# First attention stage in head pairs on 32-row groups, and projection weights issued from ScalarE's queue

## The chip, the core and the metric

The kernel runs on one core of one Trainium2 chip. The metric is the device time of one execution in microseconds (us).

## What is computed

Two blocks with a residual and a layer norm before each, on x of 16 sequences x 256 positions x 128 features. The first is causal attention with 16 heads of 8 features. The second applies 6 layers; each is windowed attention (window 32, 16 heads of 64, normalised q and k, rotary tables) and a gated feed-forward with an inner norm, both on shifted tokens.

```python
def attn(x, Wq, Wk, Wv, Wo):
    B, S, E = x.shape
    H, D = 16, 8
    proj = lambda W: jnp.einsum('bse,fe->bsf', x, W).reshape(B, S, H, D).transpose(0, 2, 1, 3)
    q, k, v = proj(Wq), proj(Wk), proj(Wv)
    s = jnp.einsum('bhsd,bhtd->bhst', q, k)
    s = jnp.where(jnp.triu(jnp.ones((S, S), dtype=bool), k=1), -jnp.inf, s)
    a = jax.nn.softmax(s / sqrt(D), axis=-1)
    out = jnp.einsum('bhst,bhtd->bhsd', a, v).transpose(0, 2, 1, 3).reshape(B, S, E)
    return jnp.einsum('bse,fe->bsf', out, Wo)

x = x + attn(layernorm(x), Wq, Wk, Wv, Wo)
y = layernorm(x)
for i in range(6):
    y = window_attn(shift(y), Wqkv[i], q_scale[i], k_scale[i], Wo[i]) + y
    y = gated_ffn(shift(y), ln_g[i], ln_b[i], W1[i], b1[i], W2[i], b2[i]) + y
x = x + y
```

## The kernel before

Each of the five engines has its own program, an order of work written out by hand, and semaphores tie them together: `need(eng, sem, value)` makes an engine wait until `sem` has reached `value`. Engines work strictly in the order of their programs. SyncE (SP) mostly issues DMAs.

**First stage.** `attention_steps` runs a pipeline over the 16 sequences. In step n, sequence n is at its head (norm, turn, projections), sequence n - 1 in the middle (scores to values), n - 2 at the tail (output, residual, norm). Steps 2 to 15 are one hardware loop. For the middle, 16 heads are taken in four groups of four, g = 0 to 3. `a_scores` puts one group's scores in PSUM: a bfloat16 matmul of the identity with the causal mask opens each of three banks (lines 1023, 1026), then for each head one matmul with the first 128 queries against 128 keys (L1030) and one with the last 128 queries against 256 keys (L1034). The stationary side is AqT, all 128 features; the moving side is KM, which holds for each head a copy of the keys with the features of the other heads set to zero. GpSimd makes KM with `spread_k` (L363) from AkT and the head mask. VectorE takes the maxima (`a_max`, L732 and L733), ScalarE the exponentials (`a_exp`, L500 and L502), TensorE turns them in 12 blocks of 128 x 512 (`a_transposes`, L1053), in two PSUM slots, and ScalarE copies blocks 0 to 5 (L513), VectorE blocks 6 to 11 (L743), to SBUF. Then come the values (`a_values`, L1063 and L1068), and `a_divide` on VectorE: transpose (L748), reciprocal, multiply over all 1024 elements (L753), transpose (L756). The output matmuls (L1075) and the residual (L761) belong to the next step. PSUM has two sets of three banks for the scores; the second also takes the values (banks 3, 4) and the output (bank 5).

For the next sequence, `a_turn` (L999), `a_x_evac` (L478), `a_project` (L1005), `a_qk_evac` (AqT at L483, AkT at L485) and `a_project_v` (L1010) stand between these. Their PSUM space is that of the two block slots, so block 3 waits for a_xe and block 4 for a_ke, the copy of AkT. TensorE's order in a step is:

```python
            def a_step(n, head, mid, tail):
...
                if head:
                    if mid:
                        need(pe, a_te, 12 * n - 12 + 3)
                    a_turn(n)
                    a_project(n)
                if mid:
                    a_scores(n - 1, 3)
                    for g in range(1, 4):
                        a_transposes(n - 1, g, head)
                    a_values(n - 1)
```

**Layers.** `stack_steps` runs the same kind of pipeline over 6 x 16 units of one sequence. At a layer's end the weights must be replaced: `load_qkv` on SyncE (L241) brings Wqkv in three parts of 512 KB, v, q and k, in the last unit's step, behind that step's `band` (L281, L283, L287) and `edge_values` (L296) DMAs, each part once s_pv, s_pq or s_pk says that the last projection with it is done. The projections are L1136; ScalarE copies their results with L568 (squares) and L575 (`keep_raw`) for q and k and L588 for v.

**Start.** SyncE issues the first inputs, weights and constants, then the load of all other inputs, and then, after GpSimd has cleared Wap, the four parts of Wap (L237). TensorE waits for all of `d_c` (5 constants) and `d_wa` (7 loads, Wap's among them) before its first instruction.

## Time and profile before

| | us |
|---|---|
| median of 3 runs (lowest to highest) | 4052.52 (4048.25 to 4054.8) |
| the profiled execution | 4053.12 |
| its span in the trace | 4051.3 |
| TensorE matmul busy | 3611.0 (89%) |
| VectorE busy | 3103.8 (77%) |
| ScalarE busy | 2876.5 (71%) |
| GpSimd busy | 2423.2 (60%) |
| first projection matmul of the layers (end of the first stage) | 544.8 |
| mean granted TensorE clock | 0.983 of full |

The span is the time from the first to the last instruction in the trace; the execution's own time is 1.8 us longer. Busy shares are means over the whole span, and a step with a chain of waits through several engines can be long while no engine in it is full. Durations of pipelined instructions overlap: what one costs in a row of its like is the distance between starts.

### The profile page before, as it was taken

The page shows a single profiled execution, that of the slowest core. Times are in us where ns is not written, and L with a number is a line of the kernel's source. Part 1 is how long each engine was busy: PE and PEld are TensorE (multiplying, and loading weights), DVE is VectorE, ACT ScalarE, POOL GpSimd, SP SyncE. Part 2 cuts the span into 40 slices and gives each one's busy share as a digit, 9 for nine tenths or more (in the row PEclk, how much of TensorE's full clock was granted, in tenths as well). Part 3 has the DMA queues.
Part 4 walks back from the last instruction along what each step waited for, and adds up shares of the span by engine and source line. Part 5 has one row for each costly group of instructions (what it writes and reads, how often), then busy time and mean ns, then how long its engine had stood idle before and what let it go on. Part 6 is the DMA issues. An engine that isn't in the chain of part 4 may idle for free.

```text
span 4051.3 us, 97145 instructions
## 1 busy us (share of the span) xinstructions
PE 3611.0 (89%) x34144; PEld 2541.3 (63%) x34144; DVE 3103.8 (77%) x5305; ACT 2876.5 (71%) x4769; POOL 2423.2 (60%) x1603
## 2 busy tenths in 40 slices
PE   6888869999889999899999899999899998999997
PEld 5666646666566666566666566666666665666665
DVE  4656658888778888778888778888788887888885
ACT  3554447777677777677777677777677776777775
POOL 3222246666666666666666666666566665667663
PEclk9999989999999999999999999999999999999998
DMA  1000001111111111111111111111211111111111
GB/s 56 0 0 0 0 12 34 32 32 34 52 41 31 35 35 35 50 38 35 35 34 36 46 42 35 34 35 35 53 35 35 34 34 44 47 35 35 34 33 48
DMA packets 183169, 136.82 MB, mean 34 GB/s; under 512 B 97612, under 2 KB 135888, under 8 KB 182992
## 3 DMA queue, kind: packets, MB, share of 16 engines
q1 hardware_dynamic: 182992, 134.51, 13.7%
q8 instruction: 104, 1.70, 0.2%
q14 instruction: 73, 0.60, 0.1%
...
## 4 chain that ended last, share of the span: by engine, by line
PE 50%; DVE 14%; ACT 11%; SPq 11%; issue 7%; DMA 5%; POOL 1%; DVEq 0%; ACTq 0%; POOLq 0%
PE ps L1136 9%; PE ps L1177 9%; PE ps L1189 8%; SPq L281 5%; PE ps L1230 5%; PE ps L1215 4%; DMA BD<-area 3%; PE ps L1204 3%; PE ps L1240 3%; SPq L283 3%; DVE area L820 3%; ACT kbd L599 2%; DVE lsum L810 2%; DVE mx L799 2%; DVE area L804 2%
## 5 line engine op out<-in xcount | busy, mean ns | idle before, releaser
L1136 PE MATMUL ps<-Wqkv,xsT 128*128 128x512 f32 x2304 | 1124.0, 611 | 93.1 <-DMA Wqkv<-ffn_Wqkv 44.5
L418 POOL TENSOR_TENSOR area<-area,tab 128x512 f32<-128x512 f32 x384 | 490.1, 1276 | 829.9 <-ACT area L575 829.9
L1136 PEld LDWEIGHTS ps<-Wqkv,xsT 128*128 128x128 f32 x2304 | 406.0, 193 | 432.8 <-issue 337.2
L432 POOL TENSOR_TENSOR area<-area,lsum 128x1024 f32<-128x1024 f32 x192 | 365.3, 1903 | 336.1 <-DVE lsum L813 336.1
L568 ACT ACTIVATE area<-ps 128x1024 f32<-128x1024 f32 x384 | 393.6, 1025 | 202.6 <-PE ps L1136 200.4
L419 POOL TENSOR_TENSOR area<-area,tab 128x512 f32<-128x512 f32 x384 | 490.0, 1276 | 0.0
L426 POOL TENSOR_TENSOR AQb<-AQb,area 128x1024 f32<-128x1024 f32 x192 | 449.8, 2365 | 7.5
L426 POOL TENSOR_TENSOR area<-area 128x1024 f32<-128x1024 f32 x192 | 450.5, 2370 | 0.0
L1177 PE MATMUL ps<-BD,area 128*64 128x128 f32 x6144 | 420.3, 279 | 20.8 <-DMA BD<-area 10.1
L1189 PEld LDWEIGHTS ps<-Wo,area 128*128 128x128 f32 x3072 | 375.9, 193 | 94.5 <-issue 93.6
L1177 PEld LDWEIGHTS ps<-BD,area 128*64 128x64 f32 x6144 | 337.3, 138 | 133.3 <-DMA BD<-area 80.1
L1129 PE MATMUL ps<-xnT,W 128*128 128x256 f32 (+1 forms) x1152 | 289.7, 388 | 120.9 <-DVE H L826 119.4
L605 ACT ACTIVATE area<-ps 128x512 f32<-128x512 f32 x384 | 210.5, 609 | 263.3 <-PE ps L1215 263.3
L575 ACT ACTIVATE area<-ps 128x1024 f32<-128x1024 f32 x384 | 392.8, 1023 | 0.0
L1230 PE MATMUL ps<-kbd,area 128*32 128x128 f32 x12288 | 377.8, 275 | 0.0
L1189 PE MATMUL ps<-Wo,area 128*128 128x128 f32 x3072 | 376.4, 276 | 1.5 <-ACT area L612 1.5
L1230 PEld LDWEIGHTS ps<-kbd,area 128*32 128x32 f32 x12288 | 325.9, 110 | 81.4 <-issue 81.3
L1129 PEld LDWEIGHTS ps<-xnT,W 128*128 128x128 f32 (+1 forms) x1152 | 198.4, 179 | 272.7 <-DVE H L826 198.3
L873 DVE TENSOR_TENSOR AQb<-area,ps 128x1024 f32<-128x1024 f32 x192 | 232.8, 1212 | 151.9 <-ACT area L575 151.9
L612 ACT ACTIVATE area<-ps 128x512 f32<-128x512 f32 x384 | 230.4, 600 | 158.6 <-PE ps L1182 113.2
L363 POOL TENSOR_TENSOR area<-AkT,headmask 128x4096 f32<-128x4096 f32 x16 | 112.4, 7027 | 373.6 <-ACT AkT L485 373.6
L820 DVE STREAM_TRANSPOSE area<-area 128x1024 f32<-128x1024 f32 x192 | 238.1, 1240 | 72.6 <-POOL area L432 72.6
...
## 6 DMA issues: line engine op xcount, KB each, us to landing
...
x2s<-x2s SPq DMA_DIRECT2D x96, 7.5 KB, 2.0
```

The source lines that it names most:

```text
L418: pool.tensor_tensor(b4[:, :, 0:h], q4[:, :, h:DH], s4[:, :, 0:h], ALU.mult).then_inc((s_bq, s_bk)[j], 1)
L419: pool.tensor_tensor(b4[:, :, h:DH], q4[:, :, 0:h], s4[:, :, h:DH], ALU.mult).then_inc((s_bq, s_bk)[j], 1)
L426: pool.tensor_tensor(AQ[t][:, col], AQ[t][:, col], BQ[:, col], ALU.add).then_inc(s_rot, 1)
L432: pool.tensor_tensor(p3, p3, lsum[:, 1, :].unsqueeze(2).broadcast_to([P, HEADS, 2 * WIN]), ALU.mult).then_inc(s_pn, 1)
L568: act.activation(SQ[:, j * INNER:(j + 1) * INNER], PJ[:, :], ACT.Square).then_inc((s_sqq, s_sqk)[j], 1)
L575: act.activation(QH[:, j * INNER:(j + 1) * INNER], PJ[:, :], ACT.Copy).then_inc((s_hq, s_hk)[j], 1)
L820: dve.transpose(PTr[t][:, :, :, :].rearrange("p b h i -> p h b i"), Pr[:, t, :]).then_inc(s_T, 1)
L1129: last = mm(TR[c % 2][0:m, half * SEQ:(half + 1) * SEQ], W1[:, half * FF + f0:half * FF + f0 + m], xnT[:, :], start=True, stop=True)
L1136: last = mm(PJ[:, b * 512:(b + 1) * 512], xsT[:, par, t * P:(t + 1) * P], Wqkv[:, w0:w0 + 512], start=True, stop=True)
L1177: last = mm(slot[DH * k:DH * k + DH, c * P:(c + 1) * P], V[par][:, t, h * DH:(h + 1) * DH], BD[:, t, :, h, :], start=(c == 0), stop=False, ...
L1189: last = mm(EXO[:, t * P:(t + 1) * P], oT[:, t, c, :], Wo[:, c, :], start=(c == 0), stop=(c == PAIRS - 1))
L1230: last = mm(SC[32 * w:32 * w + 32, c // 4, (c % 4) * P:(c % 4 + 1) * P], qT[:, c, 32 * w:32 * w + 32], kbd[:, c, :, k0:k0 + 2 * WIN], star ...
```

## The change

The first stage works on pairs of heads. The four heads of a 32-row group g are h = 4g + k, k = 0 to 3, and pair j takes head k = j // 2 of two groups, g = 2 (j % 2) and the next. Each head's score matmul contracts only the 32 rows of its group, and the two of a pair write different banks. KM therefore needs four copies instead of 16 (with `slotmask`, the head mask cut to four columns). Three sets of two banks are used in turn, values and output moving to banks 4 and 5. The mask matmul covers the 256 columns that need one. Blocks are now those of one k over the four groups; ScalarE copies four of them and VectorE eight, with a semaphore each. AqT and KM exist twice. The multiply of `a_divide` covers 8 of 32 rows of each block. Wqkv is loaded from ScalarE's program. At the start, the identity comes first, Wap and the remaining inputs later, the rotary tables last, with semaphores of their own, and GpSimd clears kbd and BD after the first KM.

```diff
-        KM = area3[:, :].rearrange("p (h k) -> p h k", h=HA)
+        KM = area3[:, 0:2048].rearrange("p (b k n) -> p b k n", b=2, k=4)
         area4 = sb("area4", [P, 2048])
         PT1 = area4[:, :].rearrange("p (h q) -> p h q", h=HA)
+        P0k = area2[:, :].rearrange("p (g k q) -> p k g q", g=4, k=4)
+        P1k = area4[:, :].rearrange("p (g k q) -> p k g q", g=4, k=4)
...
-            a_step(0, True, False, False)
-            a_step(1, True, True, False)
-            with eng.Fori(2, SEQS) as n:
-                a_step(eng.snap(n), True, True, True)
-            a_step(SEQS, False, True, True)
-            a_step(SEQS + 1, False, False, True)
-
+            a_step(0, 0, True, False, False)
+            a_step(1, 1, True, True, False)
+            with eng.Fori(0, SEQS // 2 - 1) as k:
+                for odd in range(2):
+                    a_step(eng.snap(2 * k + (2 + odd)), odd, True, True, True)
+            a_step(SEQS, 0, False, True, True)
+            a_step(SEQS + 1, 1, False, False, True)
+
+
+        PAIRS_A = HA // 2
+        TE_ACT, TE_DVE = 4, 8
+
+        def pair_bank(j):
+            return 2 * (j % 3)
+
+        def pair_heads(j):
+            return [(2 * (j % 2) + b, j // 2) for b in range(2)]
 
         def block_slot(i):
             return TR[i % 2] if i < 3 else TR[(i + 1) % 2]
 
         def block_home(i):
 
-            h = slice(i // 3 * 4, i // 3 * 4 + 4)
-            return (PT0[:, h, 0:P], PT0[:, h, P:SEQ], PT1[:, h, :])[i % 3]
+            k = i // 3
+            return (P0k[:, k, :, 0:P], P0k[:, k, :, P:SEQ], P1k[:, k, :, :])[i % 3]
+
+        def block_done(n, i):
+
+            return (a_te, TE_ACT * n + i + 1) if i < TE_ACT else (a_td, TE_DVE * n + i - TE_ACT + 1)
...
+            sp.dma_start(ident[:, :], c_ident).then_inc(d_c, 16)
             sp.dma_start(xres[:, 0:early, :], x_rows[:, 0:early, :]).then_inc(d_x, 16)
             for i, w in enumerate((wq_t, wk_t, wv_t)):
                 sp.dma_start(Wa[:, i, :], w).then_inc(d_wa, 16)
-            for src, dst in ((c_ident, ident[:, :]), (c_causal, causal_f[:, :]),
-                             (c_winmask, wmask_f[:, :, :]), (c_headmask, headmask[:, :]),
-                             (c_rot, rot[:, :, :, :])):
+            for src, dst in ((c_causal, causal_f[:, :]), (c_winmask, wmask_f[:, :, :]), (c_headmask, headmask[:, :])):
                 sp.dma_start(dst, src).then_inc(d_c, 16)
 
-            sp.dma_start(xres[:, early:, :], x_rows[:, early:, :]).then_inc(d_x2, 16)
             sp.wait_ge(i_pad, 2)
             wo_rows = wo_t.rearrange("(c g d) n -> g d c n", g=4, d=DA)
             for g in range(4):
-                sp.dma_start(Wap[32 * g:32 * g + DA, :, :], wo_rows[g]).then_inc(d_wa, 16)
-
-            def load_qkv(l, part, done):
-                col = slice(part * INNER, (part + 1) * INNER)
-                sp.dma_start(Wqkv[:, col], wqkv[l][:, col]).then_inc(done, 16)
...
-                if at == SEQS - 1:
-                    need_apart(sp, i_sp, s_pv, (layer + 1) * SEQS * TILES)
-                    load_qkv(layer + 1, 2, d_wv)
-                    need_apart(sp, i_sp, s_pq, (layer + 1) * SEQS * TILES)
-                    load_qkv(layer + 1, 0, d_wq)
-                    need_apart(sp, i_sp, s_pk, (layer + 1) * SEQS * TILES)
-                    load_qkv(layer + 1, 1, d_wk)
...
+            def spread_k(n, par):
                 need(pool, a_ke, n + 1)
-                need(pool, a_s, 4 * n)
-                pool.tensor_tensor(KM[:, :, :], AkT[:, :].unsqueeze(1).broadcast_to([P, HA, SEQ]),
-                                   headmask[:, :].unsqueeze(2).broadcast_to([P, HA, SEQ]), ALU.mult).then_inc(a_km, 1)
-
-            spread_k(0)
-            with pool.Fori(1, SEQS) as n:
-                spread_k(pool.snap(n))
+                need(pool, a_s, PAIRS_A * (n - 1))
+                pool.tensor_tensor(KM[:, par, :, :], AkT[:, :].unsqueeze(1).broadcast_to([P, 4, SEQ]),
+                                   slotmask[:, :].unsqueeze(2).broadcast_to([P, 4, SEQ]), ALU.mult).then_inc(a_km, 1)
+
+            def a_step(n, par, head, mid, tail):
+                if head:
+                    spread_k(n, par)
+                    if isinstance(n, int) and n == 0:
+                        pool.memset(kbd[:, :, :, :], 0.0).then_inc(i_zero, 1)
+                        pool.memset(BD[:, :, :, :], 0.0).then_inc(i_zero, 1)
+
+            attention_steps(pool, a_step)
...
+            def load_qkv(l, part, done):
+                col = slice(part * INNER, (part + 1) * INNER)
+                act.dma_start(Wqkv[:, col], wqkv[l][:, col]).then_inc(done, 16)
...
+            def a_exp(n, j):
+                if j == 0:
                     need(act, a_t, 12 * n)
-                need(act, a_mx, 4 * n + g + 1)
-                bank = 3 * (g % 2)
-                for h in range(4 * g, 4 * g + 4):
-                    k = h - 4 * g
-                    act.activation(E0[:, h, :], ps[:, bank, k * P:(k + 1) * P], ACT.Exp,
-                                   bias=nmx[:, 0, h:h + 1])
-                    last = act.activation(E1[:, h, :], ps[:, bank + 1 + k // 2, (k % 2) * SEQ:(k % 2 + 1) * SEQ], ACT.Exp,
-                                          bias=nmx[:, 1, h:h + 1])
+                need(act, a_mx, PAIRS_A * n + j + 1)
+                for b, (g, k) in enumerate(pair_heads(j)):
+                    h, bank = 4 * g + k, pair_bank(j) + b
+                    act.activation(E0[:, h, :], ps[:, bank, 0:P], ACT.Exp, bias=nmx[:, 0, h:h + 1])
+                    last = act.activation(E1[:, h, :], ps[:, bank, P:P + SEQ], ACT.Exp, bias=nmx[:, 1, h:h + 1])
                 last.then_inc(a_e, 1)
...
+            def a_step(n, par, head, mid, tail):
                 if mid:
                     a_exp(n - 1, 0)
+                    a_exp(n - 1, 1)
                 if tail:
                     rsqrt_guess(n - 2, b_lnc, b_lnr, b_lnr)
                 if mid:
-                    a_evac(n - 1, 0)
+                    a_exp(n - 1, 2)
+                    for i in range(3):
+                        a_evac(n - 1, i)
                 if head:
                     rsqrt_guess(n, a_lnc, a_lnr, a_lnr)
                 if mid:
-                    a_exp(n - 1, 1)
+                    a_exp(n - 1, 3)
                 if head:
                     a_x_evac(n)
                 if mid:
-                    a_exp(n - 1, 2)
-                if head:
-                    a_qk_evac(n)
-                if mid:
-                    a_evac(n - 1, 1)
-                    a_exp(n - 1, 3)
+                    a_exp(n - 1, 4)
+                if head:
+                    a_qk_evac(n, par)
+                if mid:
+                    a_evac(n - 1, 3)
+                    for j in range(5, PAIRS_A):
+                        a_exp(n - 1, j)
                 if head:
                     a_values(n)
 
             act.wait_ge(i_zero, 2)
             act.wait_ge(i_guess, 2)
+            load_qkv(0, 0, d_wq)
+            load_qkv(0, 1, d_wk)
+            load_qkv(0, 2, d_wv)
...
                     v_evac(n, 1, par)
+                    if again:
+                        load_qkv(layer + 1, 2, d_wv)
...
                     keep_raw(n, 1, 0)
+                    if again:
+                        load_qkv(layer + 1, 0, d_wq)
...
                     keep_raw(n, 1, 1)
+                    if again:
+                        load_qkv(layer + 1, 1, d_wk)
...
+            def a_max(n, j):
+
+                bank, (g, k) = pair_bank(j), pair_heads(j)[0]
+                hs = slice(4 * g + k, 4 * g + k + 5, 4)
+                need(dve, a_s, PAIRS_A * n + j + 1)
+                if j == 0:
+                    need(dve, a_e, PAIRS_A * n)
+                dve.tensor_reduce(nmx[:, 0, hs], ps[:, bank:bank + 2, 0:P], AX.X, ALU.max, negate=True)
+                dve.tensor_reduce(nmx[:, 1, hs], ps[:, bank:bank + 2, P:P + SEQ], AX.X, ALU.max, negate=True).then_inc(a_mx, 1)
+
+            def a_evac(n, i):
+
+                need(dve, a_t, 12 * n + i + 1)
+                dve.tensor_copy(block_home(i), block_slot(i).rearrange("p (h q) -> p h q", h=4)).then_inc(a_td, 1)
...
-                dve.tensor_tensor(o3, o3, Arl[:, :].unsqueeze(2).broadcast_to([P, 32, 32]), ALU.mult).then_inc(a_mu, 1)
+                heads = o3[:, :, 0:DA]
+                dve.tensor_tensor(heads, heads, Arl[:, :].unsqueeze(2).broadcast_to([P, 32, DA]), ALU.mult).then_inc(a_mu, 1)
...
+                    a_max(n - 1, 4)
+                    a_evac(n - 1, 4)
+                    a_max(n - 1, 5)
+                    a_evac(n - 1, 5)
+                    a_max(n - 1, 6)
+                    for i in range(6, 9):
+                        a_evac(n - 1, i)
+                    a_max(n - 1, 7)
+                    for i in range(9, 12):
+                        a_evac(n - 1, i)
...
+                if j >= 3:
+                    need(pe, a_e, PAIRS_A * n + j - 2)
+                bank = pair_bank(j)
                 for b in range(2):
-                    mm(ps[:, bank + 1 + b, :], ident_h[:, :], causal[:, :].unsqueeze(1).broadcast_to([P, 2, SEQ]),
-                       start=True, stop=False, skip_group_check=True)
-                for k in range(4):
-                    h = 4 * g + k
-                    mm(ps[:, bank, k * P:(k + 1) * P], AqT[:, 0:P], KM[:, h, 0:P],
-                       start=False, stop=True, skip_group_check=True)
-                for k in range(4):
-                    h = 4 * g + k
-                    last = mm(ps[:, bank + 1 + k // 2, (k % 2) * SEQ:(k % 2 + 1) * SEQ], AqT[:, P:SEQ], KM[:, h, :],
+                    mm(ps[:, bank + b, 0:3 * P].rearrange("p (a k) -> p a k", a=3)[:, 0:3:2, :], ident_h[:, :],
+                       causal[:, P:2 * P].unsqueeze(1).broadcast_to([P, 2, P]), start=True, stop=False, skip_group_check=True)
+                for b, (g, k) in enumerate(pair_heads(j)):
+                    r = slice(32 * g, 32 * g + 32)
+                    mm(ps[:, bank + b, 0:P], AqT[r, par, 0:P], KM[r, par, k, 0:P], start=False, stop=True, skip_group_check=True)
+                for b, (g, k) in enumerate(pair_heads(j)):
+                    r = slice(32 * g, 32 * g + 32)
+                    last = mm(ps[:, bank + b, P:P + SEQ], AqT[r, par, P:SEQ], KM[r, par, k, :],
                               start=False, stop=True, skip_group_check=True)
                 last.then_inc(a_s, 1)
...
+                if mid:
+                    a_scores(n - 1, 0, 1 - par)
+                    a_scores(n - 1, 1, 1 - par)
                 if tail:
                     a_output(n - 2)
                 if mid:
-                    a_scores(n - 1, 1)
+                    a_scores(n - 1, 2, 1 - par)
                     a_transposes(n - 1, 0, head)
-                    a_scores(n - 1, 2)
+                    a_scores(n - 1, 3, 1 - par)
                 if head:
                     if mid:
-                        need(pe, a_te, 12 * n - 12 + 3)
+                        need(pe, *block_done(n - 1, 2))
                     a_turn(n)
                     a_project(n)
                 if mid:
-                    a_scores(n - 1, 3)
-                    for g in range(1, 4):
-                        a_transposes(n - 1, g, head)
+                    a_scores(n - 1, 4, 1 - par)
+                    a_transposes(n - 1, 1, head)
+                    a_scores(n - 1, 5, 1 - par)
+                    a_scores(n - 1, 6, 1 - par)
+                    a_transposes(n - 1, 2, head)
+                    a_scores(n - 1, 7, 1 - par)
+                    a_transposes(n - 1, 3, head)
                     a_values(n - 1)
                 if head:
                     if mid:
-                        need(pe, a_te, 12 * n)
+                        need(pe, *block_done(n - 1, 11))
                     a_project_v(n)
```

TensorE, first stage, the step in which sequence 1 is at its head and sequence 0 in the middle, from the projections on, before (L1005 projections, L1023 to L1034 scores, L1053 block transposes, L1063 and L1068 values, L1010 projection of v):

```order
L1005 MATMUL ps<-xhT,Wa 128x256 x2
L1023 MATMUL ps<-causal,ident_h 128x512
L1026 MATMUL ps<-causal,ident_h 128x512 x2
L1030 MATMUL ps<-area,AqT 128x128 x4
L1034 MATMUL ps<-area,AqT 128x256 x4
L1053 MATMUL ps<-ident,area 128x128 x36
L1063 MATMUL ps<-area 32x256 x16
L1068 MATMUL ps<-area 32x128 x16
L1010 MATMUL ps<-Wa,xhT 128x128 x2
```

The same place in the changed kernel, from blocks 3 to 5 on (L1052 to L1059 scores of a pair, L1078 transposes, L1089 values); pair 4 stands just ahead of it:

```order
L1078 MATMUL ps<-ident,area 128x128 x12
L1052 MATMUL ps<-causal,ident_h 128x2x128 x2
L1056 MATMUL ps<-area,AqT 128x128 x2
L1059 MATMUL ps<-area,AqT 128x256 x2
L1052 MATMUL ps<-causal,ident_h 128x2x128 x2
L1056 MATMUL ps<-area,AqT 128x128 x2
L1059 MATMUL ps<-area,AqT 128x256 x2
L1078 MATMUL ps<-ident,area 128x128 x12
L1052 MATMUL ps<-causal,ident_h 128x2x128 x2
L1056 MATMUL ps<-area,AqT 128x128 x2
L1059 MATMUL ps<-area,AqT 128x256 x2
L1078 MATMUL ps<-ident,area 128x128 x12
```

Before, all scores stood ahead of the last 36 transposes; now three pairs of eight stand among them, pairs 5 and 6 behind block 5 and pair 7 behind block 8.

SyncE, the last step of a layer, before (L296 the edge values, L241 Wqkv, L302 and L303 the token shift):

```order
L296 DMA Vx<-area 32x2x128 [waits s_o]
L296 DMA Vx<-area 32x2x128 x3
L40 ISA
L241 ISA [waits s_pv]
L241 DMA Wqkv<-ffn_Wqkv 128x1024
L241 REGISTER_ALU [waits s_pq]
L241 DMA Wqkv<-ffn_Wqkv 128x1024
L241 ISA [waits s_pk]
L241 DMA Wqkv<-ffn_Wqkv 128x1024
L302 DMA x2s<-x2s 112x2x64 [waits s_r1]
L303 DMA x2s<-x2s 15x2x64
```

ScalarE, the same step in the changed kernel, around the load of q's part (L585 squares, L592 `keep_raw`, L578 gelu, L482 Wqkv):

```order
L585 ACTIVATE area<-ps 128x1024 [waits s_rq,s_pq]
L40 REGISTER_ALU
L592 ACTIVATE area<-ps 128x1024 [waits s_aq,s_bq]
L482 REGISTER_ALU
L482 DMA Wqkv<-ffn_Wqkv 128x1024
L40 REGISTER_ALU
L578 ACTIVATE G<-ps,b1s 85x256 [waits s_h]
L692 ACT_TABLE_LOAD
L585 ACTIVATE area<-ps 128x1024 [waits s_rk,s_pk]
```

The three loads have left SyncE's queue, and each now stands on ScalarE behind the copy of what the part's last matmuls wrote.

## Rows read from the trace of the kernel before

**Rows 1.** Timeline of one steady step of the first stage: start, duration, engine, line, [idle before]

```profile
151.54 1.93 PE L1063 MATMUL ps<-area 128*32 128x256 f32 x32 [0.78 <-DVE area L743]
156.08 1.22 DVE L753 TENSOR_TENSOR area<-area,Arl 128x1024 f32<-128x1024 f32 x1
161.46 0.38 PE L1023 MATMUL ps<-causal,ident_h 128*128 128x512 bf16 x1 [0.77 <-DVE x L761]
169.77 0.38 PE L999 MATMUL ps<-ident,xh 128*128 128x128 f32 x2
171.59 0.38 PE L1023 MATMUL ps<-causal,ident_h 128*128 128x512 bf16 x1
172.24 1.05 PE L1030 MATMUL ps<-area,AqT 128*128 128x128 f32 x8
173.13 1.89 PE L1034 MATMUL ps<-area,AqT 128*128 128x256 f32 x8
175.77 1.15 PE L1053 MATMUL ps<-ident,area 128*128 128x128 f32 x8 [0.31 <-ACT AkT L485]
180.18 1.09 PE L1053 MATMUL ps<-ident,area 128*128 128x128 f32 x8 [0.96 <-ACT area L502]
183.05 1.93 PE L1063 MATMUL ps<-area 128*32 128x256 f32 x32 [0.78 <-DVE area L743]
```

**Rows 2.** The same timeline: maxima, norm and exponentials in that step

```profile
165.41 0.66 DVE L732 TENSOR_REDUCE nmx<-ps 128x4 f32<-128x512 f32 x1
165.99 1.22 DVE L733 TENSOR_REDUCE nmx<-ps 128x4 f32<-128x1024 f32 x1
167.84 0.16 DVE L697 TENSOR_TENSOR lw<-lw 128x2 f32<-128x2 f32 x1 [0.64 <-ACT lw L472]
168.43 0.60 DVE L707 TENSOR_SCALAR xh<-xres,mv,lw 128x128 f32 x2
177.45 0.36 ACT L500 ACTIVATE area<-ps,nmx 128x128 f32<-128x128 f32 x1
178.06 0.38 ACT L500 ACTIVATE area<-ps,nmx 128x128 f32<-128x128 f32 x1
```

**Rows 3.** Timeline of TensorE in a layer: a change of tile shape

```profile
2020.15 0.59 PE L1225 MATMUL ps<-wmask,ident_h 128*128 128x512 bf16 x2
2020.68 1.95 PE L1230 MATMUL ps<-kbd,area 128*32 128x128 f32 x64
2022.56 1.09 PE L1215 MATMUL ps<-ident,AQb 128*128 128x128 f32 x8
...
2020.68 1.69 PEld L1230 LDWEIGHTS ps<-kbd,area 128*32 128x32 f32 x64 [0.42 <-issue]
```

**Rows 4.** First layer boundary; then all waits, landings, and a stretch with granted clock

```profile
1089.55 1.03 ACT L575 ACTIVATE area<-ps 128x1024 f32<-128x1024 f32 x1
1099.37 2.50 SPq L296 DMA_DIRECT2D Vx<-area  x4
1102.25 1.55 SPq L241 DMA_DIRECT2D Wqkv<-ffn_Wqkv  x3
1107.53 3.77 PE L1136 MATMUL ps<-Wqkv,xsT 128*128 128x512 f32 x4 [9.50 <-DMA Wqkv<-ffn_Wqkv]
1116.77 1.88 PE L1136 MATMUL ps<-Wqkv,xsT 128*128 128x512 f32 x4
...
PE ps L1136 <- DMA Wqkv<-ffn_Wqkv: 44.5, 5, 9.5
DMA to landing us min/median/max: 3.6/4.5/8.3
1107.00:1112.00 5.00, 4.47 (x9) 2.40 (x10) 0.00 (x0) 0.66 (x1) 0.00 (x0) 0.50 0.20 79
```

**Rows 5.** The start: timeline

```profile
16.66 0.66 PE L999 MATMUL ps<-ident,xh 128*128 128x128 f32 x2 [16.66 <-DMA Wap<-Wo_t]
20.70 7.02 POOL L363 TENSOR_TENSOR area<-AkT,headmask 128x4096 f32<-128x4096 f32 x1 [8.71 <-ACT AkT L485]
```

119 lines of the change are left out of this document (48 added, 71 removed).

## The prediction

> **What bounds the kernel now.** I read the page first: the first stage, which most of the diff touches, ends at about 544 of 4051 us. TensorE is the busiest engine, but what matters for a reordered stage is what it waits for, so I went to the timeline of one steady step of the first stage. One step runs from the start of the value matmuls at 151.54 to the same place at 183.05, 31.5 us [rows 1]. In it TensorE works through four score groups of 3.4 us (mask 171.59 to the end 173.13 + 1.89) and stands still where a wait ends last: for the residual at 161.46, for ScalarE's AkT at 175.77, for exponentials at 180.18, for a block copy at 183.05 [rows 1]. So the step is a chain through three engines. The second place is a layer boundary: the projection matmuls wait 44.5 us in five waits for Wqkv [rows 4]. The third is the start, where TensorE waits until 16.66 for the last Wap load [rows 5].
>
> Below, t counts from the start of the value matmuls of a step.
>
> **Cost of a pair of heads.** Before, a group of four heads has three mask matmuls (171.59 to 172.24, 0.65), four 128-column ones (to 173.13, 0.89) and four 256-column ones (1.89 with 0.17 of pipeline end, so 0.43 per head) [rows 1]. A pair now has one 512-column mask's worth of work in two halves, 0.21, then 2 x 0.22 and 2 x 0.43. The rows of before show no row group of 32, only column groups: 64 instructions (two per f32 matmul) in 1.95, about 28 ns each, where a 128-column instruction of the score group takes 110 (0.89 for eight): four run side by side [rows 1, 3]. If the two row groups do too, the multiplying takes 0.22 + 0.43 = 0.65. The weight loads may then bind: 64 loads of 32 columns took 1.69, 26 ns each, one behind the other [rows 3]; eight loads of 128 columns at four times that take 0.85. Changing the shape costs 0.53 - 0.43 = 0.10 on the way in (2020.15 to 2020.68 with two masks of 0.21) and about 0.15 on the way out (64 x 0.0267 after 2020.68 is 2022.39, the next starts at 2022.56) [rows 3]. Bounds of a pair: below, everything beside everything, 0.21 + 0.65 = 0.86 with free switches, 0.95 with the way in; above, nothing side by side, 0.21 + 0.10 + 0.44 + 0.86 = 1.6. I take 1.2, near the bound by loads (0.21 + 0.10 + 0.85 + the end of the last matmul), because loads are what the nearest rows show to be serial.
>
> A rule of the Trainium skill (TensorEngine Tiling, Tiling Modes) says that changing the tiling mode drains the engine; the 0.10 and 0.15 agree with it. By the page TensorE: Matmul & The Clock Gate, section LDWEIGHTS, a 32x128 load takes as long as a 128x128 one, an estimate of 107 ns x 8 = 0.86 here; the sum by it would be a pair of 1.27 and 5 us more in all.
>
> **Other new durations.** A reduce over 512 elements takes 0.58 until the next starts and one over 1024 takes 1.22, 1.1 ns an element [rows 2]; the new ones over 256 and 512 take 0.33 + 0.58 + 0.08 of end = 1.0 per pair. Exponentials take 0.61 per head (177.45 to 178.06), so 1.2 per pair and 0.1 of end [rows 2]. Newton and normalising take 1.2 (167.84 to 169.03), a block's copy of 512 elements is taken like the reduce, 0.6 [rows 2]. The multiply of the division shrinks from 1024 to 256 elements: 1.22 to 0.40 [rows 1].
>
> **The step, link by link.**
> 1. Values, division, output, residual: 161.46 - 151.54 = 9.9 before; the shorter multiply makes it 9.1. That multiply is on the path.
> 2. Pair 2 waits for this (its banks hold the output): end at 10.5, maxima 11.45, exponentials 12.8. ScalarE now has them ahead of the copy of block 0, so block 2 can be transposed only at 13.4, until 13.95.
> 3. Pair 3: end 15.4, maxima 16.3, normalising 17.5 (it stands behind this maximum on VectorE), then turn, copy, projections: 2.0, as from 169.77 to the mask at 171.59 with its load [rows 1]. t = 19.55; before 20.05.
> 4. Pair 4: end 20.95, maxima 21.9, exponentials 23.2, AqT and AkT 23.85, and block 4 starts at 23.9. Before, it started at 175.77, t = 24.2. Up to here nothing is lost.
> 5. Before, one group had yet to be exponentiated, and all scores were done; values began 7.3 later. Now pairs 5, 6 and 7 are still to be computed. Blocks 4 and 5 end at 24.9; pair 5 at 26.3, maxima 27.3, exponentials 28.75. Pair 6 hides beside these. Blocks 6 to 8 end at 30.8 (each waits for the copy two before it).
> 6. Pair 7 stands behind them on TensorE: end 32.25, maxima 33.2, exponentials 34.65. Blocks 9 to 11 and the last copy take 183.05 - 180.18 = 2.9 as before [rows 1]. Values at t = 37.5.
>
> So a step takes 6.0 us more, though TensorE computes 4 us less in it. With 16 sequences there are 15 such intervals: **+90**. Five pairs lie on the path, so 0.1 us on a pair is 0.5 on a step and 8 in all.
>
> **Start.** KM of 7.02 [rows 5] is computed over a quarter of the elements, 1.8: -5.2, once; in the steady step it ends long before it is needed, so doubling q and keys buys nothing there. TensorE waited for Wap until 16.66 [rows 5]; the new order needs only ident, the masks and three weights, so it can start when VectorE has normalised the first sequence. But ScalarE's 1.5 MB of Wqkv now run beside them. I take -4.5 (bounds 0 and -7). The later load of the other inputs is needed in step 1, some 25 us in: nothing. The memsets of kbd and BD move behind the first KM on GpSimd, beside idle time.
>
> **Layer boundaries.** SyncE issues all three Wqkv loads at 1102.25, behind a step's band and edge DMAs, and q's matmuls start at 1107.53 after 9.5 us of waiting, in a stretch with a granted clock of 0.50 (1.2 GHz): four instructions take 3.77 there and 1.88 in the next such place [rows 4]. On ScalarE, q's load is issued behind the copy of q's raw projection, 1089.55 + 1.03 = 1090.6; with 0.5 for the issue (three took 1.55) and 4.5 to landing it is there at 1095.6, and TensorE is ready for it at 1107.53 - 9.50 = 1098.0 [rows 4]. k's comes some 5 us later and is needed after another 6 us of matmuls. That gives back 44.5 + 5 x 1.9 = 54. The 15 issues now cost ScalarE up to 0.5 each, 7.8 in all, some of it on its path to TensorE: 4. **-50**, bounds -35 (landing at the slowest 8.3 [rows 4], issues fully seen) and -58 (the rest of those steps freed too).
>
> **Sum** against the profiled execution's 4053.1: +90 - 5.2 - 4.5 - 50 = +30, or 4083. The median of the runs, 4052.5, is the same within 0.02%. About 0.2%, 8 us, is what a measurement of this kernel can tell from no change.
>
> **Rivals.**
> - *TensorE's work decides, not the chain* (ends faster). Place: from block 4 to the values. Four groups of 3.4 become eight pairs of 1.2, 4.1 us less a step, if the maxima and exponentials of pairs 5 and 7 are hidden: 4053 - 62 - 60 = 3931. It decides against me from a lengthening under 4.0 us a step (60 / 15). For it: TensorE is the busiest engine. Against it: TensorE already waits there with only one group left, and each pair must pass two more engines. 8%, with the intermediate sizes.
> - *The row groups do not run side by side*: a pair is 1.6, a step 2.2 longer again, 4083 + 33 = 4116. For it: no row shows row groups. Against it: column groups do overlap. 14%.
> - *The loads come no earlier from ScalarE's queue.* Each boundary keeps its 9.5 us: 4083 + 50 = 4133. Against it: SyncE reached them straight from the edge loads (1099.37 + 2.50, then 1102.25) [rows 4], while their conditions had long been met; the wait is its order. The Trainium skill (Trainium Kernel Development and Optimization, Key Constraints) says that issuing from several engines saves only the sequencer's issue time; here that would be some 1.5 us a boundary. 4%.
> - *The change does only its small parts*, pairs at the lower bound and boundaries fully freed: 4083 - 20 - 8 - 3 = 4052, no change. 8%, with its neighbours.
> - My forecast, slower by 0.3 to 1.2%: 66%.
>
> The range, 4046 to 4121, takes in the lower bounds together and the rival of the row groups; outside lie most of the first rival and the third. Faster by over 0.2%: 0.11 (the first rival and 3 from the low end of the forecast); within: 0.10 (the fourth and 2 more); slower: 0.79.
>
> **What would show it.** A steady step of 36.5 to 38.5 between value matmuls, its length added after block 4; TensorE waiting 2.5 us before blocks 6 and 9 for exponentials; a pair of 1.0 to 1.3 on TensorE; no wait for Wqkv at the boundaries, the first projection at 11 to 13 us. I am wrong if a step stays under 35.5, or if Wqkv is still waited for.

## The result, and the profile after

The changed kernel took 4197.86 us (median of 4 runs, 4192.29 to 4205.28). The kernel before, on the same chip, took 4053.66 (4048.25 to 4059.97). The ratio is 1.0356, with a 95% interval from 1.0334 to 1.0378: slower by 144 us. Forecast were 4083 us and a range of 4046 to 4121. The direction was right, the size was not, and the time lies outside the range.

The profiled execution spans 4190.5 us. Its page begins so (busy time of each engine; then the span in 40 slices, PEclk being the granted clock in tenths):

```profile
span 4190.5 us, 97397 instructions
...
PE 3677.9 (88%) x34208; PEld 2530.5 (60%) x34208; DVE 3122.3 (75%) x5465; ACT 2868.7 (68%) x4737; POOL 2342.3 (56%) x1607
...
PE   6767767799999899998999989999989999999997
...
PEclk9777776899999999999999999999999999999998
```

Of the first seven slices of PEclk, some 730 us, the first reads 9, five read 7 and the last 6; behind them stand 8 and 9. These seven are the first stage. To see where it ends in each trace, take the first projection of the layers:

```profile
L1168 PE MATMUL ps<-Wqkv,xsT 128*128 128x512 f32 x2304 | 1121.0, 610 | 48.0 <-ACT area L592 43.6 <-ACT area L605 3.3 <-ACT xsT L567 1.0
```

The timeline gives this line's first start as 738.9 us, where before it was 544.8. So the account of the profiled executions is: first stage **+194.1**, layers 4190.5 - 738.9 = 3451.6 against 4051.3 - 544.8 = 3506.5, **-54.9**. The sum, +139.2, is what the two spans differ by.

**The layers.** In the row above no time is left behind a Wqkv transfer, where [rows 4] had 44.5 us. The loads now come from ScalarE's queue (from the view of the tile Wqkv):

```profile
L482 ACTq DMA_DIRECT2D Wqkv<-ffn_Wqkv x18: 345/357/453, 2.0 to 3560.9; - x18
```

The first boundary step, from the first matmul of one unit (the transpose of its input, L1145; L1113 before) to that of the next, takes 36.56 us (1219.42 to 1255.98), where before it was 47.0 (1095.60 to 1142.59): 10.4 saved; there are five boundaries.

**The first stage.** One steady step on TensorE, from the start of the value matmuls (the timeline: start, time, instruction, and in brackets the idle time before it and what ended it). It answers to [rows 1]:

```profile
151.25 3.55 PE L1089 MATMUL ps<-area 128*32 128x256 f32 x32 [0.88 <-DVE area L762]
...
156.16 0.38 PE L1052 MATMUL ps<-causal,ident_h 128*128 128x256 bf16 x2
156.47 0.49 PE L1056 MATMUL ps<-area,AqT 32*128 32x128 f32 x4
156.79 0.60 PE L1059 MATMUL ps<-area,AqT 32*128 32x256 f32 x4
157.32 0.39 PE L1052 MATMUL ps<-causal,ident_h 128*128 128x256 bf16 x2
...
162.00 0.39 PE L1052 MATMUL ps<-causal,ident_h 128*128 128x256 bf16 x2 [0.78 <-DVE x L781]
...
166.25 0.66 PE L1078 MATMUL ps<-ident,area 128*128 128x128 f32 x4 [1.98 <-ACT area L523]
...
170.20 0.69 PE L1028 MATMUL ps<-ident,xh 128*128 128x128 f32 x2 [2.22 <-DVE xh L731]
171.36 2.07 PE L1034 MATMUL ps<-xhT,Wa 128*128 128x256 f32 x4 [0.47 <-ACT xhT L495]
...
178.38 1.93 PE L1078 MATMUL ps<-ident,area 128*128 128x128 f32 x8 [2.48 <-ACT AkT L502]
...
184.68 2.56 PE L1078 MATMUL ps<-ident,area 128*128 128x128 f32 x12 [1.34 <-ACT area L517]
...
191.76 3.02 PE L1078 MATMUL ps<-ident,area 128*128 128x128 f32 x12 [2.52 <-ACT area L517]
...
195.66 0.65 PE L1089 MATMUL ps<-area 128*32 128x256 f32 x4 [0.88 <-DVE area L762]
```

The step is 195.66 - 151.25 = **44.4 us**, against 31.5 before and the 37.5 of the prediction. The starts of the value matmuls divide the stage's +194.1 in this way: -7.1 until the first score matmul (it starts at 20.72, and at 27.78 before), +11.9 from there to the first values (these start at 61.78, and at 56.97 before), +188.3 in the fifteen intervals between the first and the last values (the last one is shorter in both kernels and grew by 7.6 only), and +0.9 from the last values to the layers. Two things are to be seen in the step. Most waits have the places and the sizes of the prediction's walk: 2.52 us for exponentials before block 9, 2.48 for AkT before block 4. And instructions that the change did not touch take up to twice as long: the value matmuls 3.55 where they took 1.93 [rows 1], the eight transposes of blocks 4 and 5 1.93 where eight at full clock take 1.09 (163.18 in this same step), the projections 2.07 where they take 1.13 in the experiments below. The table by stretch says why (stretch, its length, busy time and instructions of PE, PEld, DVE, ACT and POOL, the granted clock, DMA share, GB/s):

```profile
151.25:155.00 3.75, 3.75 (x48) 2.15 (x52) 0.00 (x0) 0.00 (x0) 0.00 (x0) 0.56 0.02 4
155.00:160.00 5.00, 4.40 (x58) 3.04 (x48) 4.15 (x7) 0.38 (x1) 0.00 (x0) 1.00 0.01 2
160.00:165.00 5.00, 3.49 (x29) 2.52 (x28) 3.71 (x14) 3.84 (x13) 0.00 (x0) 1.00 0.00 0
165.00:170.00 5.00, 1.73 (x14) 1.10 (x14) 2.92 (x13) 3.68 (x12) 0.00 (x0) 0.82 0.00 0
170.00:175.00 5.00, 4.33 (x16) 2.69 (x16) 0.14 (x1) 0.82 (x3) 0.00 (x0) 0.50 0.00 0
175.00:180.00 5.00, 2.52 (x16) 2.04 (x13) 1.53 (x3) 2.39 (x7) 1.51 (x1) 0.84 0.00 0
...
185.00:190.00 5.00, 4.23 (x22) 2.64 (x19) 2.78 (x5) 1.16 (x4) 0.00 (x0) 0.53 0.00 0
190.00:195.70 5.70, 3.06 (x16) 2.36 (x19) 2.40 (x4) 1.36 (x4) 0.00 (x0) 0.50 0.00 0
```

The granted clock is 1.00 (2.4 GHz) from 155 to 165, where TensorE works without a long break. Then it waits 1.98 and 2.22 us, and from 170 to 175 the clock is 0.50 (1.2 GHz). It comes back, and is gone again from 185 on, into the value matmuls of the next step (the first line shows that place one step earlier). Before, the four stretches of 50 us from 50 to 250 all had 1.00. In the change such stretches have 0.70 to 0.76 from 100 us on, the lowest and the highest of them being:

```profile
100.00:150.00 50.00, 34.21 (x234) 22.82 (x230) 22.72 (x51) 16.54 (x48) 1.89 (x1) 0.70 0.00 0
...
200.00:250.00 50.00, 36.10 (x262) 24.19 (x258) 25.49 (x55) 16.76 (x49) 1.89 (x1) 0.76 0.00 0
```

**The start.** TensorE's first instruction comes at 14.72, against 16.66 [rows 5]. It no longer waits for Wap but for VectorE, which begins its part only when the last constant has landed. The copy of keys on GpSimd takes 1.89 against 7.02 [rows 5]:

```profile
11.35 0.23 DVE L736 CAST ident_h<-ident 128x128 bf16<-128x128 f32 x1 [11.35 <-DMA headmask<-const]
...
14.72 0.66 PE L1028 MATMUL ps<-ident,xh 128*128 128x128 f32 x2 [14.72 <-DVE xh L731]
...
18.77 1.89 POOL L370 TENSOR_TENSOR area<-AkT,slotmask 128x1024 f32<-128x1024 f32 x1 [6.34 <-ACT AkT L502]
```

### The profile page after: what moved, and what is told of

Same layout as the page of the kernel before. It is cut to its first block, busy times and chain, and to the rows that moved or that the text cites. A ratio compares the mean times of both kernels' runs of the same rounds, so it can differ in the third digit from the quotient of the medians.

```text
span 4190.5 us, 97397 instructions
## 1 busy us (share of the span) xinstructions
PE 3677.9 (88%) x34208; PEld 2530.5 (60%) x34208; DVE 3122.3 (75%) x5465; ACT 2868.7 (68%) x4737; POOL 2342.3 (56%) x1607
## 4 chain that ended last, share of the span: by engine, by line
PE 55%; DVE 15%; ACT 11%; SPq 7%; issue 7%; DMA 4%; POOL 1%; ACTq 0%; DVEq 0%; POOLq 0%
PE ps L1168 10%; PE ps L1209 9%; PE ps L1221 8%; PE ps L1262 5%; SPq L291 4%; PE ps L1236 4%; DMA BD<-area 4%; PE ps L1247 3%; PE ps L1272 3%; PE ps L1078 3%; SPq L293 2%; DVE area L849 2%; DVE lsum L839 2%; ACT kbd L616 2%; DVE mx L828 2%
## 5 line engine op out<-in xcount | busy, mean ns | idle before, releaser
L585 ACT ACTIVATE area<-ps 128x1024 f32<-128x1024 f32 x384 | 393.5, 1025 | 156.5 <-PE ps L1168 154.2
L592 ACT ACTIVATE area<-ps 128x1024 f32<-128x1024 f32 x384 | 392.6, 1022 | 0.0
L370 POOL TENSOR_TENSOR area<-AkT,slotmask 128x1024 f32<-128x1024 f32 x16 | 30.3, 1894 | 618.4 <-ACT AkT L502 618.4
L516 ACT ACTIVATE area<-ps,nmx 128x128 f32<-128x128 f32 x256 | 95.0, 371 | 303.9 <-DVE nmx L757 303.9
```

The lines of the kernel that those rows point to most:

```text
L585: act.activation(SQ[:, j * INNER:(j + 1) * INNER], PJ[:, :], ACT.Square).then_inc((s_sqq, s_sqk)[j], 1)
L592: act.activation(QH[:, j * INNER:(j + 1) * INNER], PJ[:, :], ACT.Copy).then_inc((s_hq, s_hk)[j], 1)
```

## The experiments

The question is what made a step 44.4 us and not 37.5, and what each other part was worth. Theories on the step, named in the expectations by letters: a longer chain with the lost clock on top; more work or slower work of TensorE itself (the 32-row form); something else in the new parts. Then: is it the form of the score matmuls or the order around them that costs, and can the order be mended?

### The weight loads alone

The kernel before, with only the issue of Wqkv moved to ScalarE's program: the three first loads ahead of its first stage, the others each behind ScalarE's copy of the last projection of their part.

```diff
-                if at == SEQS - 1:
-                    need_apart(sp, i_sp, s_pv, (layer + 1) * SEQS * TILES)
-                    load_qkv(layer + 1, 2, d_wv)
...
+                    v_evac(n, 1, par)
+                    if again:
+                        load_qkv(layer + 1, 2, d_wv)
...
+                    keep_raw(n, 1, 0)
+                    if again:
+                        load_qkv(layer + 1, 0, d_wq)
```

> The kernel before, with only the Wqkv loads moved to ScalarE's program. Theory A (loads issued earlier): the layers give back what they gave back in the changed kernel, 3506.5 to 3451.6 us, so about 55 us: 3995 to 4002 us, no wait of TensorE for Wqkv, first stage unchanged with 31.5 us a step. Rival (the gain of the layers came from something else in the change, such as the rotary tables or the clearing of BD): 4045 to 4055 us.

Measured: 4001.47 us (3993.4 to 4002.19), ratio 0.9878, interval 0.9862 to 0.9895. The profiled span is 3999.5, the first stage ends at 545.0, so the layers take 3454.5: **-52.0** of the change's -54.9. The steady step stays at 31.5. This part is a gain by itself, and the loss of the change is all in the rest. This is the time that the expectation gave. TensorE starts at 18.19 here, 1.5 later than in [rows 5], with 1.5 MB of Wqkv beside the first loads; the last experiments return to it. The first values come at 56.98, where they came at 56.97 before: matmuls near 30 us reached full clock sooner in this execution, and that hid the later start.

### Filling TensorE's waits

The changed kernel, with idle work for TensorE: 39 mask matmuls of 128 x 512 per step, into banks that are overwritten later, issued where it would wait (8 before block 2, 8 before the turn, 9 before block 4, 4 before block 6, 10 before block 9). They add work and take nothing away, so if this kernel is faster, the clock is what is left to explain it.

```diff
+            def fill(n, pairs, bank, count):
+                need(pe, a_e, PAIRS_A * n + pairs)
+                for _ in range(count):
+                    mm(ps[:, bank, :], ident_h[:, :], causal[:, P:2 * P].unsqueeze(1).broadcast_to([P, 4, P]),
+                       start=True, stop=True, skip_group_check=True)
...
+                if k == 2:
+                    fill(n, 5, 2, 4)
+                if k == 3:
+                    fill(n, 6, 4, 10)
...
+                    if i == 2:
+                        fill(n, 2, 2, 8)
+                    if i == 4:
+                        fill(n, 3, 4, 9)
...
+                        fill(n - 1, 2, 2, 8)
                         need(pe, *block_done(n - 1, 2))
```

> The changed kernel with 39 extra bfloat16 matmuls of the mask a step, placed in TensorE's five long waits of the first stage and written to banks that are free there. Theory B (the waits of the longer chain let the clock fall to half, and the half clock adds the 7 us a step that the forecast lacks): the granted clock stays at 1.00, a steady step takes 36.5 to 38.5 us although TensorE has 8 us more to do in it, and the time falls by about 15 x 7 = 105, to 4080 to 4110 us. Rival C (the clock falls because of the 32-row matmuls): granted clock stays near 0.7, a step takes 44 us or more, 4190 us or more. Rival D (the pair itself costs more): clock 1.00 but a step of 42 us or more.

Measured: 4077.5 us (4071.31 to 4081.01), ratio to the kernel before 1.007, interval 1.0053 to 1.0087. So 8 us of added matmuls a step made the changed kernel some 116 us faster (by the ratios; 120 by the medians). Its table by stretch, and a step on its timeline:

```profile
150.00:200.00 50.00, 43.58 (x340) 26.09 (x339) 27.38 (x60) 20.25 (x59) 3.79 (x2) 1.00 0.00 0
```

```profile
167.67 1.93 PE L1103 MATMUL ps<-area 128*32 128x256 f32 x32 [0.88 <-DVE area L762]
...
191.11 1.14 PE L1092 MATMUL ps<-ident,area 128*128 128x128 f32 x8 [0.53 <-ACT AkT L502]
...
198.94 2.33 PE L1066 MATMUL ps<-causal,ident_h 128*128 128x512 bf16 x10
201.53 1.09 PE L1092 MATMUL ps<-ident,area 128*128 128x128 f32 x8 [0.25 <-ACT area L517]
...
204.50 1.93 PE L1103 MATMUL ps<-area 128*32 128x256 f32 x32 [0.88 <-DVE area L762]
```

The granted clock is 1.00, the value matmuls are back at 1.93, and the step is 204.50 - 167.67 = 36.8 us, as expected (36.5 to 38.5; the total fell slightly below the expected 4080). The wait before block 9 is still there, only now it is filled: 2.33 us of added matmuls and 0.25 of waiting. So of the 12.9 us that a step grew, **5.3 are the longer chain and 7.6 the half clock**. Over the whole stage, which ends at 623.4 here, 78.6 of the 194.1 us are left and 115.5 came from the clock. This kernel is also a test of the prediction's walk, since it runs at the clock that the walk assumed. From the start of the value matmuls, in us:

| start of | walk | filled | the change |
|---|---|---|---|
| pair 2 | 9.1 | 9.1 | 10.8 |
| block 2 | 13.4 | 13.3 | 15.0 |
| turn | 17.5 | 17.3 | 19.0 |
| pair 4 | 19.55 | 19.2 | 22.0 |
| block 4 | 23.9 | 23.4 | 27.1 |
| block 6 | 28.75 | 28.2 | 33.4 |
| pair 7 | 30.8 | 30.1 | 35.8 |
| block 9 | 34.65 | 33.9 | 40.5 |
| next values | 37.5 | 36.8 | 44.4 |

No link of the walk is off by more than 0.8 us. The last column departs from the second wherever TensorE's own instructions lie on the chain.

### The score matmuls over 128 rows

The changed kernel with the stationary and moving sides of the score matmuls over all 128 rows. The computation is changed: KM of the change holds two masked copies in each row group, so a matmul over all rows sums four heads, and the scores are not those of the reference.

```diff
-    mm(ps[:, bank + b, 0:P], AqT[r, par, 0:P], KM[r, par, k, 0:P], start
+    mm(ps[:, bank + b, 0:P], AqT[:, par, 0:P], KM[:, par, k, 0:P], start
-    last = mm(ps[:, bank + b, P:P + SEQ], AqT[r, par, P:SEQ], KM[r, par, k, :],
+    last = mm(ps[:, bank + b, P:P + SEQ], AqT[:, par, P:SEQ], KM[:, par, k, :],
```

> The changed kernel with score matmuls over all 128 rows instead of 32; this changes the computation, each head's scores now contain the sum of the products of four heads. Theory B: the waits stay, so the clock stays low (0.65 to 0.8), and a step takes 44 to 48 us, as each pair is about 0.4 us longer and nothing else changes. Rival C (32-row matmuls do not keep the clock up): the clock is 0.95 or more and a step takes 38 to 40 us.

Measured, in a single execution: 4189.85 us, a step of 44.5 (190.21 to 234.67), first stage to 732.9. The step is as the expectation had it; the clock came out above its 0.65 to 0.8, and under the 0.95 of its rival. The pair costs more, and the clock is better:

```profile
195.41 0.38 PE L1052 MATMUL ps<-causal,ident_h 128*128 128x256 bf16 x2
195.63 0.61 PE L1056 MATMUL ps<-area,AqT 128*128 128x128 f32 x4
196.07 1.03 PE L1059 MATMUL ps<-area,AqT 128*128 128x256 f32 x4
196.94 0.38 PE L1052 MATMUL ps<-causal,ident_h 128*128 128x256 bf16 x2
```

```profile
200.00:250.00 50.00, 34.70 (x241) 27.35 (x240) 24.06 (x62) 19.17 (x58) 1.89 (x1) 0.86 0.00 0
```

A pair is 1.53 us (195.41 to 196.94), where the 32-row one is 1.16 (156.16 to 157.32 in the trace of the change). The granted clock in stretches of 50 us from 100 on is 0.81 to 0.86, where the change has 0.70 to 0.76. Slower matmuls at a better clock make the same step. So the 32-row form, which computes faster, bought the change's steady step nothing: the time saved became waiting, and with it went clock. The run also speaks against the form itself as what slows the stage: without it the step is just as long.

### A new order for the three engines

The changed kernel with the steps of TensorE, ScalarE and VectorE in another order, and the blocks shared out differently between the two copying engines. The idea is that every pair is computed as early as its banks allow, the head of the next sequence sits between the pairs, and the transposes come last, so that no engine has a run of work that another waits for.

```diff
-        TE_ACT, TE_DVE = 4, 8
+        BY_ACT, BY_DVE = [0, 1, 2, 4, 5, 9, 11], [3, 6, 7, 8, 10]
+        PE_ORDER = ("sc0 sc1 out sc2 tr0 sc3 tr1 tr2 sc4 sc5 turn sc6 proj tr3 sc7 tr4 tr5 tr6 tr7 tr8 tr9 tr10 tr11 val projv").split()
+        ACT_ORDER = ("exp0 exp1 rsb ev0 exp2 ev1 rsa ev2 exp3 xe exp4 exp5 qk exp6 ev4 ev5 exp7 ev9 ev11 ve").split()
+        DVE_ORDER = ("max0 max1 res max2 newtb moma max3 newta max4 max5 max6 ev3 max7 ev6 ev7 ev8 ev10 div").split()
```

> The changed kernel with the same work in the first stage, but another order on TensorE, ScalarE and VectorE: pairs 3 to 6 ahead of the transposes that wait for exponentials, no engine's queue blocked by a late step, and seven blocks copied by ScalarE. Theory E (order alone makes the stage slow, pairs themselves are cheap): by laying the measured durations end to end a step takes 26 to 28 us with the clock at 1.00, so 15 x 17 us less than the changed kernel: 3925 to 3955 us, faster than the kernel before by 2.5 to 3%. Rival C: clock near 0.7, a step of 32 us or more, 4010 us or more.

Measured: **3901.06 us** (3893.07 to 3909.61), ratio to the kernel before 0.963, interval 0.9612 to 0.9647. The first stage ends at 453.6, 91 us earlier than in the kernel before.

```profile
153.73 1.93 PE L1076 MATMUL ps<-area 128*32 128x256 f32 x32 [0.76 <-ACT area L533]
...
173.21 1.07 PE L1065 MATMUL ps<-ident,area 128*128 128x128 f32 x8
174.85 1.14 PE L1065 MATMUL ps<-ident,area 128*128 128x128 f32 x8 [0.57 <-ACT area L533]
176.29 1.25 PE L1065 MATMUL ps<-ident,area 128*128 128x128 f32 x8 [0.30 <-DVE area L762]
177.73 1.16 PE L1065 MATMUL ps<-ident,area 128*128 128x128 f32 x8 [0.19 <-DVE area L762]
179.65 1.72 PE L1076 MATMUL ps<-area 128*32 128x256 f32 x28 [0.76 <-ACT area L533]
```

```profile
150.00:200.00 50.00, 44.13 (x429) 30.23 (x428) 35.44 (x88) 30.89 (x90) 2.68 (x2) 1.00 0.00 0
```

The step is 25.9 us and was expected at 26 to 28. TensorE waits less than a microsecond at any place in it, and the clock is 1.00. TensorE does the same work a step as in the change; all that differs is when. The total came out below the expected 3925 to 3955. The stage of the profiled execution is 285 us shorter than the change's, where 15 x 17 = 255 were expected, as the steady step fell by 18.4 and not 17; the profiled execution took 3909.61, the slowest of the four.

### Only TensorE's new order

To see whether TensorE's order alone does it: TensorE as above, ScalarE and VectorE in the order of the change, blocks shared out as in the change.

```diff
+        BY_ACT, BY_DVE = [0, 1, 2, 3], [4, 5, 6, 7, 8, 9, 10, 11]
+        ACT_ORDER = ("exp0 exp1 rsb exp2 ev0 ev1 ev2 rsa exp3 xe exp4 qk ev3 exp5 exp6 exp7 ve").split()
+        DVE_ORDER = ("max0 max1 res max2 newtb moma max3 newta max4 ev4 max5 ev5 max6 ev6 ev7 ev8 max7 ev9 ev10 ev11 div").split()
```

> The changed kernel with TensorE's order of the new order alone; ScalarE and VectorE keep the order of the changed kernel. Theory E (TensorE's late pairs 5, 6 and 7 are the larger part of the longer chain): laying the durations end to end gives a step of 32.5 us at full clock, against 36.9 measured with filled waits and 25.9 with all three orders new. If the clock then stays up, 4198 - 15 x 11.9 = 4020 us; if it still falls in part, up to 4090 us. Rival F (the orders of ScalarE and VectorE hold the step, TensorE's alone changes nothing): 4150 us or more.

Measured: 4062.4 us (10 runs, 4051.26 to 4073.87), ratio 1.0007, interval 0.9992 to 1.0021: no difference from the kernel before, and within the 4020 to 4090 of the theory. This and the later experiments ran on other chips than those above. The kernel before took 4059.21 us beside this one and 4049.8 beside the new order, so kernels from different chips are compared by their ratios to it. By these (1.0356 - 1.0007) the change is 141 us slower than this kernel. The steps alternate: 34.35, 36.65, 35.5, 36.8 and 34.35 from 126.23 to 303.93. The stage ends at 606.8. The granted clock of a stretch lies between the two levels (0.74 to 0.89 for 50 us), and the long waits that are left stand before block transposes, for ScalarE's exponentials (L527):

```profile
200.00:250.00 50.00, 38.50 (x343) 26.34 (x332) 29.83 (x73) 21.77 (x63) 1.89 (x1) 0.86 0.00 0
...
225.00:230.00 5.00, 1.90 (x10) 1.50 (x9) 1.73 (x5) 1.35 (x4) 0.00 (x0) 0.50 0.00 0
```

```profile
228.79 3.07 PE L1065 MATMUL ps<-ident,area 128*128 128x128 f32 x12 [3.10 <-ACT area L527]
```

With the order of TensorE mended, a step still has a wait of 3.10 us for ScalarE's exponentials, and TensorE computes at half clock behind it: the twelve transposes take 3.07. TensorE's order is worth some 140 us on the change, the order of the other two engines on top of it another 150 (1.0007 - 0.963). What the other two orders do without TensorE's was not run.

### The new order with 128-row scores

The edit of the third experiment on the kernel with the new order (again the scores are sums over four heads).

> The new order with score matmuls over all 128 rows; this changes the computation, each head's scores contain the sum of the products of four heads. The pair costs 1.53 us in place of 1.17 (both measured back to back at full clock). Theory G (32-row groups save TensorE 0.36 us a pair, and in the new order part of it shows): a step of 27.5 to 28.5 us against 25.95, 3925 to 3940 us. Rival (the chain hides it): 25.9 to 26.5 us a step, 3900 to 3910 us.

Measured, in a single execution: 3915.77 us, steps of 27.15 (127.52, 154.70, 181.82) at a granted clock of 1.00, between what the theory and its rival had given. Here the 32-row form is worth 1.2 us a step, 18 in all by the steps. It is a gain once TensorE's work lies on the path; eight times the 0.37 by which a pair is shorter would be 3.0, so part of it is hidden even then.

### The new order with one q and one KM

The new order with AqT and KM single again. Their copies then wait until the last pair of the sequence before has been computed.

```diff
-                need(act, a_s, PAIRS_A * (n - 1))
-                act.activation(AqT[:, par, :]
+                need(act, a_s, PAIRS_A * n)
+                act.activation(AqT[:, 0, :]
...
-                need(pool, a_s, PAIRS_A * (n - 1))
-                pool.tensor_tensor(KM[:, par, :, :]
+                need(pool, a_s, PAIRS_A * n)
+                pool.tensor_tensor(KM[:, 0, :, :]
```

> The new order with one AqT and one KM instead of two, each then written only when all eight pairs of the sequence before are done. Theory (the doubling is worth little once the order is right): 26.8 us a step by laying durations end to end, 13 us in all, 3910 to 3918 us. Rival (doubling makes the order possible): 29 us a step or more, 3950 us or more.

Measured: 3928.16 us (3919.21 to 3932.76), ratio 0.9677, interval 0.9661 to 0.9693. Steps alternate between 27.84 and 26.77, the clock is 0.97 to 0.99. The plain difference to 3901.06 is 27 us, but the two were timed on different chips. By the ratios (0.9677 - 0.963) the doubling is worth 19 us, give or take some 10, and by the profiles 18 in the fifteen intervals (405.6 against 387.7 from the first to the last values): at or just above the 9 to 17 that were expected. In this order TensorE's projections of the next sequence stand ahead of the last pair ("proj tr3 sc7"); with a single tile the copy of q must wait for that pair.

### The first weights later

The new order, where ScalarE issues the first three Wqkv loads (needed only some 450 us later) after the constants have landed.

```diff
             act.wait_ge(i_guess, 2)
+            act.wait_ge(d_c, 16 * N_CONST)
             load_qkv(0, 0, d_wq)
```

> The new order, with ScalarE issuing the first three Wqkv loads only when the constants have landed. Theory H (at the start the constants landed late, at 11.35 us, because 1.5 MB of Wqkv ran beside them): VectorE starts at 7 to 8 us and TensorE at 10.5 to 11.5 us instead of 14.7. Rival (they are late because of their place in SyncE's queue): TensorE still starts at 14 us or later.

Measured, in a single execution: 3899.74 us.

```profile
6.08 0.23 DVE L737 CAST ident_h<-ident 128x128 bf16<-128x128 f32 x1 [6.08 <-DMA headmask<-const]
...
9.57 0.66 PE L1017 MATMUL ps<-ident,xh 128*128 128x128 f32 x2 [9.57 <-DVE xh L732]
```

The last constant lands at 6.08 and TensorE starts at 9.57, earlier than the theory had said; in the kernel with the new order these are 12.15 and 15.54. So the 1.5 MB beside them had delayed the last of the small first loads by 6 us. The stage ends at 443.3 against 453.6.

The same kernel was timed in six executions.

> The version with the new order and ScalarE's first Wqkv loads behind the constants, this time timed against the kernel before. The new order alone gave a ratio of 0.963; TensorE's start came 6.0 us earlier in the single look (9.57 against 15.54). Theory: the whole of it shows, a ratio near 0.961 and 3895 to 3905 us. Rival (the late weights give it back at the start of the layers, or the start is hidden): a ratio of 0.963 or above.

Measured: 3899.11 us (3888.44 to 3932.12), ratio 0.9645, interval 0.9614 to 0.9676. The median is where the theory had it, the ratio where the rival had it; one of the six took 3932.12 with a mean granted clock of 0.938, the others 3888.44 to 3901.67 with 0.987 to 0.990. The interval overlaps that of the new order alone, so whether the total gains stays open. The profiles show how much of a shorter stage is the loads. In two executions of this kernel it ends at 443.3 and 446.4, 10.3 and 7.1 us before the new order's. TensorE starts 6.0 us earlier in both; from its start to the first values it takes 30.0 and 34.5 us, and 34.4 in the new order's trace, because the first matmuls have doubled durations for a longer or a shorter time. The 6.0 are due to the edit; the rest differs between two executions of one kernel. Either version is the best found here: some 150 us below the kernel before and, by the ratios, 290 below the change.

## Why the prediction was wrong in its size

The direction held, and so did the mechanism that gave it, a chain through three engines that grows when pairs stand between the late transposes. The boundary term held too. The sum failed in the term for the step, which is mis-sized.

**The +90 for the step.** *So a step takes 6.0 us more* is the step that failed. A steady step took 12.9 more, and the fifteen intervals grew by 188.3 where +90 was forecast. The walk itself was good: at full clock a step grew by 5.3 (filled waits), and no link was off by over 0.8. With filled waits the whole stage grew by 78.6, where the prediction's three terms for it (+90, -5.2, -4.5) give 80.3; that these agree so closely is in part luck, since the fifteen intervals grew by 79.5 there, the stretch from the first scores to the first values, which the prediction did not count, by another 6.7, and the start gave 6.9 and not 9.7. What it left out is that every duration in it was taken from rows with a granted clock of 1.00, and that the new waits, which it listed, change the clock. The runs put this at 7.6 us a step and 115.5 in the whole stage. The hint was there: the prediction quoted projections of 3.77 us at a granted clock of 0.50 behind a wait of 9.5 [rows 4], priced it at the boundaries, and did not ask what several waits of about 2 us and more a step (it named two of 2.5) would do in a stage where the kernel before has none of over 1 us in a steady step. By the Trainium skill (TensorE: Matmul & The Clock Gate, The HAM clock gate), half clock is TensorE's resting state and its own activity releases it; filling the waits agrees with this, with 0.70 to 0.76 in the change and 1.00 with them filled.

**Rivals.** *TensorE's work decides* did not come about in the change: it waits for the other two engines more than before. But its time, 3931, is about what the same matmuls give in another order (3901). *The row groups do not run side by side* is refuted: a pair is 1.16 us back to back, where 1.2 was taken and 1.6 was the upper bound (by its own 0.4 a pair the rival's 33 us should be 30). *The loads come no earlier* is refuted: -52.0 alone, -54.9 in the change. The rule of the Trainium skill quoted there (Trainium Kernel Development and Optimization, Key Constraints), that several issuing engines save only issue time, would have given back at most 7.5 us in five boundaries, an estimate from the prediction's 1.5 each. The measured 52 differ from it: what cost here was the place of the loads in SyncE's order.

**The small terms.** Layer boundaries: -50 forecast, -54.9 measured, within its bounds. The 2.9 us between that and the experiment with the loads alone are within what the same layers scatter by: over the nine profiled experiments they take 3446.4 to 3455.2 us. Start: -4.5 forecast, TensorE started 1.9 earlier. The effect that the prediction named, Wqkv beside the first loads, was larger than it allowed: with Wqkv held back, TensorE starts 5.97 us earlier. KM: 1.8 forecast, 1.89 measured. The two together put the first score matmul 7.1 us earlier, where 9.7 were forecast. *Doubling q and keys buys nothing there* looked at the length of KM alone. Single tiles were not run in the order of the change, but its program shows that they would not work there: ScalarE's copy of q would wait for pair 7, pair 7 stands behind block 4 on TensorE, and block 4 waits for AkT, whose copy stands behind that of q. In the new order the doubling is worth some 19 us.

**The range.** It covered the lower bounds and slow row groups, but no case in which TensorE's durations themselves change. The trace had the price: durations doubled at 0.50 [rows 4]. Behind the new waits of the filled step lie turn and projections (1.9), pair 4 (1.2), blocks 4 and 5 (1.0), blocks 6 to 8 (1.6), pair 7 (1.2), blocks 9 to 11 (1.5), and values with what follows to the first pair (3.3), 11.7 us at full clock, short waits included. Doubled, they would make the walk's 37.5 a step of 49 us, an estimate from these rows, and the measured 44.4 lies between the two. A range up to half clock everywhere would have been wide, but right about what was not known.

Of the signs named in advance, the wait before block 9 (2.5 said, 2.52 measured), the pair, and the missing wait for Wqkv came as said. Others did not, or only in part: the step (36.5 to 38.5 said); its length added after block 4 (2.9 of the 12.9 us are there when block 4 starts, at 27.1 against 24.2 before); the wait before block 6 (2.5 said, 1.34 measured; the walk itself leaves little over 1 us there, as pair 6 fills the rest); and the first projection (11 to 13 said, 15.86 measured, TensorE's first instruction at 14.72).
